# The scaling of the second norm, moved from VectorE to ScalarE

## The reference, cut to what matters

```
x = x + attention(layernorm(x))      # 16 heads of 16, linear attention, causal
x = x + experts(layernorm(x))        # 8 experts of 256-512-256, top 2 per token
layernorm(x) = (x - mean(x)) / sqrt(var(x) + 1e-5)
```

## Time and profile before

| | |
|---|---|
| runs | 1280.41, 1280.44, 1289.2 us; median 1280.44 |
| profiled execution | span 1283.9 us from first to last instruction; no other time of it is given |
| busy | PE 1022.5 (80%), PEld 805.4 (63%), DVE 832.9 (65%), POOL 694.4 (54%), ACT 663.9 (52%) |
| mean granted TensorE clock | 0.918 of full speed |
| attention part | to about 690 us; the experts after it |

### The profile page before, as it was taken

How to read it: one execution, slowest core, us unless ns; L and a number is a source line. 1 busy time by engine, 2 the same in 40 slices (tenths; PEclk the granted TensorE clock), 3 DMA queues, 4 the chain that set the end, 5 groups by cost and what they waited for, 6 DMA issues and landing times.

```text
span 1283.9 us, 32900 instructions
## 1 busy us (share of the span) xinstructions
PE 1022.5 (80%) x10045; PEld 805.4 (63%) x10046; DVE 832.9 (65%) x2225; ACT 663.9 (52%) x1253; POOL 694.4 (54%) x603
## 2 busy tenths in 40 slices
PE   4699988889888988888881888787888888887872
PEld 2477766567666766656761776676666666666661
DVE  4488889978888889899876454444444444444441
ACT  5576656667676666766532544343343333333340
POOL 5544756777667766777736244444444444443444
PEclk9899988999898989999985899999899899998996
DMA  3748553566554655545536344444444444443343
GB/s 94 181 116 199 141 136 102 144 153 156 124 143 123 156 141 123 131 133 137 136 129 235 71 75 69 67 66 66 66 66 66 66 66 66 66 67 65 66 62 37
DMA packets 125061, 138.18 MB, mean 108 GB/s; under 512 B 10304, under 2 KB 118208, under 8 KB 124352
## 3 DMA queue, kind: packets, MB, share of 16 engines
q1 hardware_dynamic: 97216, 100.53, 32.5%
q0 software_dynamic: 26592, 35.67, 15.4%
q10 hardware_dynamic: 1184, 1.18, 0.3%
HBM read 72.00 MB, written 65.34 MB: 107 GB/s over the span
## 4 chain that ended last, share of the span: by engine, by line
DMA 27%; issue 22%; DVE 22%; PE 17%; POOL 5%; ACT 2%; another core or an unknown queue 2%; POOLq 1%; SPq 1%; DVEq 1%; ACTq 0%
DMA out<-yt,to_token 25%; DVE ahl L1026 5%; PE pF L421 4%; PE pO L517 2%; PE pA L421 2%; POOL out L1474 2%; PE pS L493 2%; PE pS L496 2%; DVE xn L1121 2%; POOL expert_in L1401 1%; DVE v L1086 1%; PE pR L559 1%; DVE xn L1122 1%; ACT ahl L785 1%
## 5 line engine op out<-in xcount | busy, mean ns | idle before, releaser
L1474 POOL DMA_INDIRECT out<-yt,to_token x142 | 227.0, 1598 | 101.0 <-POOL to_token L1469 58.0
L785 ACT ACTIVATE ahl<-pS 128x512 f16<-128x512 f32 x240 | 141.5, 600 | 111.3 <-PE pS L496 106.0
L1026 DVE SCALAR_TENSOR_TENSOR ahl<-pS,ahl 128x512 f16<-128x512 f32 x240 | 161.2, 681 | 26.5 <-ACT ahl L785 25.9
L1401 POOL DMA_INDIRECT expert_in<-xn,cur x128 | 130.1, 1016 | 35.2 <-issue 33.3
L421 PE MATMUL pS<-gT,w1s 128*128 128x256 f16 x864 | 109.0, 286 | 41.0 <-DVE gT L1314 40.8
L1469 POOL COPY to_token<-row_token 128x2 int32 (+1 forms) x71 | 14.2, 200 | 233.1 <-DMA out<-yt,to_token 225.2
L953 ACT ACTIVATE g<-pS,b1s 128x256 f32<-128x256 f32 x144 | 60.3, 471 | 147.8 <-PE pS L421 147.8
L421 PEld LDWEIGHTS pS<-gT,w1s 128*128 x864 | 85.8, 102 | 63.5 <-issue 49.9
L493 PE MATMUL pS<-cbs 128*128 128x512 bf16 x240 | 94.6, 394 | 33.6 <-DVE ahl L1026 26.1
L1342 DVE SCALAR_TENSOR_TENSOR yt<-pU,b2s 128x512 f32<-128x512 f32 x36 | 24.9, 692 | 142.7 <-DMA out<-yt,to_token 140.5
L421 PE MATMUL pF<-xT,was 128*128 128x512 f16 x384 | 106.6, 421 | 10.8 <-DVE xT L1031 10.7
(11 more groups left out here) (155 smaller groups left out, 2466.2 us busy)
## 6 DMA issues: line engine op xcount, KB each, us to landing
xg<-expert_in SPq DMA_DIRECT2D x71, 260.0 KB
qk_parts<-qkhl SPq DMA_DIRECT2D x32, 512.0 KB, 2.9
qst<-qk_parts SPq DMA_DIRECT2D x96, 128.0 KB
kst<-qk_parts SPq DMA_DIRECT2D x48, 256.0 KB
xs<-x SPq DMA_DIRECT2D x16, 512.0 KB
xr<-x SPq DMA_DIRECT2D x16, 512.0 KB, 4.7
out<-x SPq DMA_DIRECT2D x16, 512.0 KB
expert_in<-pads SPq DMA_DIRECT2D x16, 260.0 KB, 6.2
```

Source lines behind the costliest of these rows:

```text
L785: nc.scalar.activation(ahl[:, b % 2, 0, n * 4 * C:(n + 1) * 4 * C], score_bank(fr, n)[:], ACT.Relu).then_inc(sc_hi, 1)
L1026: V.scalar_tensor_tensor(ahl[:, b % 2, 1, cols], score_bank(fr, n)[:], 0.0, ahl[:, b % 2, 0, cols], ALU.max, ALU.subtract).then_inc(sc_lo, 1)
L1401: G.indirect_dma_start(xg_dram, bass.IndirectOffsetOnAxis(ap=cur[:, qp, 2 * b + t:2 * b + t + 1], axis=0), xn2[:, qp, b], None).then_inc(s ...
L1474: G.indirect_dma_start(out, bass.IndirectOffsetOnAxis(ap=to_token[:, c % 2, s:s + 1], axis=0), yt[:, c % 2, s], None, compute_op=ALU.add). ...
```

## The change

`norm2_apply` moves from VectorE's body into ScalarE's. There it computes `rs2 * x1 + sh2`, with the reciprocal root rs2 as scale and a new tile sh2 as bias; both hold one number per token. sh2 = -mean * rs2 is made by a new VectorE operation over all 4 batches, `norm2_shift`, where the first scalings stood. The semaphore ln2_sh tells ScalarE that it is ready. ScalarE takes over the wait for the scatters that read the buffer's last content; VectorE gets a wait for the scalings of the step before.

```diff
+        sh2 = sb("sh2", [P, B], F32, att)
@@ ScalarE
+                def norm2_apply(b):
+                    if b == 0:
+                        act.wait_ge(ln2_sh, r + 1)
+                        if c >= 4:
+                            act.wait_ge(scat_out[c % 2], 128 * front_of(j, c - 2)[1])
+                    nc.scalar.activation(xn2[:, c % 2, b, 0:D], x1[:, b], ACT.Identity, bias=sh2[:, b:b + 1],
+                                         scale=rs2[:, b:b + 1]).then_inc(xn2_done, 1)
...
                 if c == STEPS + 1:
+                    for b in range(B):
+                        norm2_apply(b)
                     w2_high(0)
                     w2_high(1)
...
                 if fr:
                     feature_exp(2)
                     qk_high(1)
+                if ro and c < STEPS:
+                    norm2_apply(0)
+                    norm2_apply(1)
                 if bk:
                     out_hi(s, 0)
                     score_hi(1, 2)
+                if ro and c < STEPS:
+                    norm2_apply(2)
+                    norm2_apply(3)
+                if bk:
                     score_hi(1, 3)
+                if c == STEPS:
+                    for b in range(B):
+                        norm2_apply(b)
                 if ro:
                     row_copy(0)
@@ VectorE
-                def norm2_apply(b):
-                    if b == 0:
-                        dve.wait_ge(ln2_rs, r + 1)
-                        if c >= 4:
-                            dve.wait_ge(scat_out[rp], 128 * rh)
-                    V.tensor_scalar(xn2[:, rp, b, 0:D], x1[:, b], mv2[:, b, 0:1], rs2[:, b:b + 1], ALU.subtract,
-                                    ALU.mult).then_inc(xn2_done, 1)
+                def norm2_shift():
+                    dve.wait_ge(ln2_rs, r + 1)
+                    if c != 2:
+                        dve.wait_ge(xn2_done, 4 * r)
+                    V.scalar_tensor_tensor(sh2[:], mv2[:, :, 0], -1.0, rs2[:], ALU.mult, ALU.mult).then_inc(ln2_sh, 1)
...
                     router_slots()
-                    for b in range(B):
-                        norm2_apply(b)
+                    norm2_shift()
                 else:
                     if bk:
                         score_lo(1, 1)
                     if ro:
-                        norm2_apply(0)
-                        norm2_apply(1)
+                        norm2_shift()
                     if bk:
                         out_lo(s, 0)
                         score_lo(1, 2)
-                    if ro:
-                        norm2_apply(2)
-                        norm2_apply(3)
                     if bk:
                         score_lo(1, 3)
```

More of the change, by code:

```diff
@@ L222, in build @@
         ln1_sh = sem("ln1_sh")
-        ln2_st, ln2_mv, ln2_ve, ln2_rs = sem("ln2_st"), sem("ln2_mv"), sem("ln2_ve"), sem("ln2_rs")
+        ln2_st, ln2_mv, ln2_ve, ln2_rs, ln2_sh = sem("ln2_st"), sem("ln2_mv"), sem("ln2_ve"), sem("ln2_rs"), sem("ln2_sh")
         xn_done, xr_in, xr_done = sem("xn_done"), sem("xr_in"), sem("xr_done")
```

## The result

The changed kernel takes **1291.97 us** (median of 20 runs, 1281.03 to 1304.16) against 1282.65 for the kernel before, run in turn with it on the same chip (20 runs, 1271.9 to 1296.03): a ratio of **1.0069, 95% interval 1.0040 to 1.0097**, 8.9 us slower. Repeated on another chip it was 1.0107 (1.0077 to 1.0137). The forecast was 1293, 13 us above the 1280.44 known then; measured were 9 us on the first chip and 13 on the second.

The account below looks back on a forecast made before the run. VectorE and TensorE were taken to share the bound in the attention steps. Terms of 10 (ordinary steps), 0.4 and 2.5 us (last two calls) gave +13 us on the 1280.44 median: 1293 us; forecast's own range 1284 to 1302, 8-in-10 range 1276 to 1310.

Parts of the forecast that it names:

- The place in ScalarE's queue: Attention steps: scalings ahead of ScalarE's copies make it the local bound, +4 to +22 us in all; chance 0.55.
- The walk: The 14 ordinary attention steps, each delay worked out from its own profile rows: sum 10 us, bounds none and 29 us.
- VectorE's relief buys nothing: Ordinary steps: the 2.9 us taken from VectorE gain nothing, as VectorE then waits for ScalarE instead.
- the second kind of step: Six steps where ScalarE was early but the shift waits for GpSimd: +0.5 or +1.4 us each, 5.5 together.
- The rival "faster": Attention steps: VectorE's relief makes steps earlier and ScalarE's work falls into its waits for TensorE: -10 to -14 us; chance 0.13.
- the rival on the port: Shift held for a whole GpSimd operation nearly every step, with TensorE's clock lower after longer idling: 29 us or more; chance 0.15.
- The swallowing by the remote wait: Late in each step VectorE's 1.5 us remote wait takes up the delay: only +1 to +5 us remain; chance 0.17.
- The tail: Last call: scalings ahead of two weight splits delay the router's chain by 4.7 us; 2.5 taken, bounds 1 and 4.7.
- the first of the two last calls: Four ScalarE activations before the router copy take 2.1 instead of 1.38 us, plus 0.17 for the shift: +0.4 us.
- The rule of the Trainium skill: Adds and multiplies belong on VectorE: moving the 64 scalings would cost 10 us; the prediction said place decides instead.

Follow-up runs that it names:

- the idle products in both kernels: Three unneeded TensorE products ahead of row 0's projection, where TensorE waits for VectorE's aT: added to the changed kernel 1.0012, added to the kernel before 0.9903.
- The relief alone: Kernel before with VectorE's scalings cut to 16 of 256 columns and nothing added on ScalarE; it computes something else: 1274.94 us, ratio 0.9887.
- the shift is early: Changed kernel with VectorE's shift moved ahead of the low part of score (1, 0), ScalarE's order unaltered: 1274.08 us, 0.9937 times the kernel before.
- the hand-over with nothing taken off VectorE: Kernel before, keeping VectorE's scalings, plus the small VectorE operation and four idle ScalarE activations, the first waiting for it: 1308.68 us, ratio 1.0174.
- the version in the gaps: Changed kernel with shift early, ScalarE's scalings ahead of scores (1, 1) and (2, 1), tail weight splits ahead of scalings, row-by-row residual waits: 1268.19 us, ratio 0.9883.
- idle ScalarE work without the wait: Kernel before, keeping VectorE's scalings, plus four idle ScalarE activations at the change's places in 13 of 14 ordinary steps: 1280.94 us, ratio 0.9992.
- the first group: Four kernels run on one chip: idle ScalarE work added 0.9992, scalings on ScalarE cut to 16 columns 0.9928, shift early 0.9937, shift early in the gaps 0.9883.

## Why the number was right, and what in its working was wrong

**The place in ScalarE's queue: right in kind, and near in size.** The steps were to grow by 0.75 to 1.1 us in most cases between the shift and row 1. Row 0 to row 1 grew by 0.92 on the mean, in after's two profiles alike, and the router product came 4.01 us behind the shift in the median step, where 3.95 was worked out (258.2 - 254.25). The walk gave 10 us for 14 steps. The profiles show 18.8 and 18.5: 0.92 x 14 = 12.9 up to row 1, and most of the rest between row 1 and row 2 (0.3 and 0.6 us a step), which the walk took as unchanged. With the idle products in both kernels, where the low pieces are nearly equal (13 and 16), the 14 steps differ by 559.1 - 550.0 = 9.1 us, and the times by 1.1% of 1288, 14 us.

**"VectorE's relief buys nothing": wrong.** This is the step that failed. The relief alone is worth 1.1% of the time. It shows again when the shift is early: 0.6% faster than before with the same work on the same engines as in the changed kernel. The 10 us were thus not a delay with nothing against it, but the net of a larger one and a gain. The two halves measured singly agree with that: +1.7% for the hand-over with nothing taken off VectorE and -1.1% for the relief add up to +0.6%, where the change measured +0.7 and +1.1%. The shift held ScalarE up where ScalarE had been ready, and with it the copies behind; undone, 1.3 to 1.7% come back. I had seen that ScalarE was early in the second kind of step, six of the 14, and costed the delay from the shift on, but did not ask what an earlier shift would give. The rival "faster" named the right point, ScalarE's readiness; its 10 to 14 us are about what the version in the gaps gained, 1.2% or 15 us.

**The clock: left out of the forecast, and part of the loss.** It stood only in the rival on the port. Over all executions on one chip the mean granted clock was 0.911 for after (11 runs) and 0.920 for before (22 runs), and within each kernel a clock lower by 0.01 goes with a time longer by 7.4 and 5.9 us. So 0.008 is 5 to 6 of the 14.4 us between their means, and 8 to 9 are left for the order of work. That is a correlation, no separation of the two. That idle products at one place take low pieces away, and that the time falls with them, the runs show. It is not the sum of TensorE's idle time that counts: idle ScalarE work without the wait leaves it idle 79 us in the 14 steps with 19 pieces, the changed kernel 74 us with 29. The additional pieces lie for the most part behind row 0 (10 and 14 there instead of 4), where the change delays the chain. Which of the waits there makes the difference stays **open**, since the one I filled is in both kernels. That the forecast's number came out is partly luck: a gain and a loss were left out, of similar size.

**The port: did not come, as its chance of 0.15 had it.** The small operation took 0.15 to 0.27 us in all but three of the 14 steps, and over 1 us in two. In these two GpSimd's operation had begun just before, and the small one ended with it, as in the earlier trace rows; in the others GpSimd's began after it, with it, or was about to end.

**The swallowing by the remote wait: wrong for the changed kernel.** The wait kept its 1.5 us. It is not a constant of the step, though: it is missing in the four profiles of the first group, with the shift early and at the change's place alike, and row 2 to 3 takes 7.1 to 7.2 us there instead of 5.9. In these four the small router operation stands behind a GpSimd addition and ends with it, as here with the shift early (306.23 + 2.37 = 308.60, 306.74 + 1.90 = 308.64):

```profile
306.23 2.37 POOL L1378 TENSOR_TENSOR xr<-xr,bos 128x1024 f32<-128x1024 f32 x1
...
306.74 1.90 DVE L1130 TENSOR_TENSOR pd<-mx 128x4 f32<-128x4 f32 x1
```

**The tail: the chain right, its worth not.** 4.7 us were worked out for the router's chain, 4.6 measured. Of the 2.5 us taken for the end, 0.7 arrived in the two profiles, which is less than profiles of one tail differ. GpSimd's last block of scatters starts 45.8 us after the last row-0 division instead of 44.0, 1.9 us later where "about 1" was said (the prediction's own numbers give 4.7 - 3.2 = 1.5), with a gap of 2.16 us ahead of it; but its last scatter starts 57.2 us after that division in both kernels. In the first of the two last calls the terms written there add up to 0.6 us (2.1 - 1.38 + 0.17 - 0.3), not 0.4; no run measures it.

**The rule of the Trainium skill** that multiplies belong on VectorE (ScalarE: Activation LUTs, Rules for kernel authors) would by itself have kept the scalings where they were. For the time of one instruction the traces agree with it: 0.50 us from start to start on ScalarE against 0.35 on VectorE. For the kernel it did not decide: with the same activations and the shift early, the kernel with them on ScalarE is faster than before by 0.6 to 1.2%.

## What to carry to other kernels

When work moves from a full engine to one with room, ask first what the receiver waits for at that place and what stands behind it in its queue: here a 0.15 us operation made 2.7 us later stood between a gain of 0.6% and a loss of 0.7 to 1.1% (on different chips). Cost the relief and the delay each by itself, since a net that comes out right can hide two wrong terms. And before a distance in one profile is set beside that in another, look whether a wait like the remote one is in both. Where TensorE idles in short pieces, compare its busy time for the same number of products before reading a longer step as a longer chain.

## What was not expected of the hardware

Three idle products of 0.22 us in a wait of 0.78 us took 1% off two different kernels and put 0.8% or more on where there was no wait; TensorE did 42 products more in 13.5 us less busy time, at 0.96 instead of 0.91 of its clock. In before and after the low pieces came behind groups of idle times of 0.3 to 1.1 us as well as behind, or with, single ones of 2 to 3.6 us. And VectorE waited 1.5 us for TensorE's result for row 2 in nearly every step of ten profiles, behind the recorded end of the product, and in no step of four others.
